# Graph attention layers on one Trainium2 core: the softmax weights move from the one-hots into the gathered rows and the edge features

## The reference

```python
def _gat_layer(x, src, dst, edge_attr_full, W, att, b, ew, eb):
    edge_emb = edge_attr_full @ ew.T + eb
    xw = x @ W
    xj = xw[src].reshape(-1, H, D) + edge_emb.reshape(-1, H, D)
    xi = xw[dst].reshape(-1, H, D)
    ...
    alpha = ea / (denom[dst] + EPS)
    msg = xj * alpha[..., None]
    aggr = jax.ops.segment_sum(msg, dst, num_segments=N)
    return aggr.mean(axis=1) + b
```

## Time and profile before

| | |
|---|---|
| time, median of 3 runs | 5991.09 us (5987.72 to 5996.44) |
| span of the profiled execution | 6300.0 us |
| PE busy | 5130.7 us, 81% |
| PE weight loads busy | 4275.1 us, 68% |
| DVE busy | 4152.4 us, 66% |
| ACT busy | 3248.8 us, 52% |
| POOL busy | 2967.6 us, 47% |
| the five attention layers | about 1790 to 4130 us of the span |

### The profile page before, as it was taken

One profiled execution on the slowest core, in us unless ns is written; L12 is line 12 of the kernel. 1 busy time (PEld: TensorE's weight loads), 2 busy tenths in 40 slices (PEclk: granted clock), 3 DMA queues, 4 the chain that ended last, 5 costly groups with the idle time before them and its releaser, 6 DMA issues. The chain is left out here.

```text
span 6300.0 us, 105600 instructions
## 1 busy us (share of the span) xinstructions
PE 5130.7 (81%) x29899; PEld 4275.1 (68%) x29899; DVE 4152.4 (66%) x16499; ACT 3248.8 (52%) x8537; POOL 2967.6 (47%) x2871
## 2 busy tenths in 40 slices
PE   4888998889959969969969969977795757758655
PEld 3666666667749959959959958844575646646555
DVE  4666776678856657757757757778475647737754
ACT  1667777777735535535535535534573325646400
POOL 1655665555564334334334335312561346545366
PEclk6999999999979979979979979955897768989855
DMA  2988776555535435535535535458573446745332
GB/s 72 176 182 185 193 191 189 185 186 196 192 100 119 109 68 118 110 67 116 113 66 115 113 69 122 110 171 250 130 155 80 137 117 187 206 108 113 65 86 79
DMA packets 1227633, 841.35 MB, mean 134 GB/s; under 512 B 335962, under 2 KB 1188542, under 8 KB 1226736
## 3 DMA queue, kind: packets, MB, share of 16 engines
q1 hardware_dynamic: 1146756, 706.02, 43.4%
q0 software_dynamic: 77040, 128.08, 9.5%
q10 hardware_dynamic: 3264, 0.50, 0.0%
HBM read 390.57 MB, written 448.11 MB: 133 GB/s over the span
## 5 line engine op out<-in xcount | busy, mean ns | idle before, releaser
L747 POOL DMA_INDIRECT gat_G<-table,k_src_row x980 | 958.2, 978 | 903.8 <-PE gat_psE L1515 688.5
L1437 ACT ACTIVATE gat_aggT<-gat_psG 128x512 f32<-128x512 f32 x490 | 292.5, 597 | 656.5 <-PE gat_psE L1515 573.2
L1510 PE MATMUL gat_psG<-gat_S,gat_G 128*128 128x256 f32 x1960 | 602.8, 390 | 31.4 <-issue 19.8
L1515 PE MATMUL gat_psE<-gat_S,gat_exr 128*128 128x128 f32 x3920 | 607.3, 278 | 0.0
L451 POOL TENSOR_TENSOR nodes_rstd<-nodes_var,k_half 128x14 f32<-128x14 f32 x138 | 360.4, 2612 | 517.8 <-DVE nodes_var L511 514.4
L1302 DVE TENSOR_SCALAR gat_S<-k_iota,k_endpos,gat_al 128x128 f32<-128x128 f32 x1960 | 551.0, 342 | 59.0 <-issue 38.4
L1515 PEld LDWEIGHTS gat_psE<-gat_S,gat_exr 128*128 128x128 f32 x3920 | 524.5, 195 | 0.0
L1526 PE MATMUL gat_psZ<-gat_aggT,t_gat_wh 128*128 128x256 f32 x1960 | 508.3, 382 | 2.7 <-ACT gat_hT L1444 1.3
L1512 PE MATMUL gat_psG<-k_ident,gat_loop 128*128 128x128 f32 x1960 | 379.6, 276 | 0.0
L1526 PEld LDWEIGHTS gat_psZ<-gat_aggT,t_gat_wh 128*128 128x128 f32 x1960 | 336.4, 192 | 32.0 <-ACT gat_aggT L1437 2.9
L1444 ACT ACTIVATE gat_hT<-gat_psZ,t_gat_bias 128x256 f32<-128x256 f32 x490 | 231.9, 473 | 239.1 <-issue 137.0
(11 more groups left out here) (650 smaller groups left out, 14567.1 us busy)
## 6 DMA issues: line engine op xcount, KB each, us to landing
table<-nodes_rows SPq DMA_DIRECT2D x660, 198.0 KB
table<-nodes_n SPq DMA_DIRECT2D x396, 192.0 KB
gat_own<-table SPq DMA_DIRECT2D x490, 132.0 KB
table<-gat_rows SPq DMA_DIRECT2D x392, 132.0 KB
nodes_x<-in_x SPq DMA_DIRECT2D x132, 192.0 KB
out<-nodes_x_out SPq DMA_DIRECT2D x132, 192.0 KB
gat_exr<-in_ex_pad SPq DMA_DIRECT2D x70, 336.0 KB
gat_G<-table,k_src_row POOLq DMA_INDIRECT x980
```

The costliest lines, as they stand in the source:

```text
L747: eng.indirect_dma_start(to, None, table, bass.IndirectOffsetOnAxis(ap=index, axis=0)).then_inc(sem, 16)
L1437: eng.activation(aggT[:, i % RA, :, :, :].rearrange("p t h q -> p (t h q)"), psG[i % 2][:, :], ACT.Copy).then_inc(s.aggT, 1)
L1510: eng.matmul(o, G[:, g % RG, c, 0:D], S[:, i % RS, t, :, :].rearrange("p h q -> p (h q)"), start=True, stop=False)
L1515: mm = eng.matmul(psE[i % 2][:, t * P:(t + 1) * P], exr[:, g % 2, c, (1 - h) * EDGE_F:(1 - h) * EDGE_F + P], S[:, i % RS, t, h, :], start= ...
```

## The change

The one-hot of a tile, `ends_at`, no longer carries the weight and is made once for both heads; a pair's two come from one DVE instruction of 128x256. The weights are multiplied into the gathered rows instead (`Gw`, one DVE instruction of 128x512 a pair: two tiles, two heads) and, once a group, into the edge features (`wex`, one DVE instruction of 128x448, in `weighed_features`, issued ahead of the group's first pair). A tile's two heads stand side by side in the 32 columns of `wex`, so one product of 128 columns replaces the two on the edge features. On the rows, two products of 128 columns (one a head, each with its own stationary `Gw`) replace the one of 256. The edge features are loaded into a tile of their own, `ex`, which is contiguous in a partition; its buffer comes free when `wex` has been computed, and `wex` itself when the group before last has been aggregated. The first `aggregate` of a group waits for `wex` rather than for the load.

```diff
-        exr = A.sb("exr", [P, 2, GM, P + EDGE_F])
-        S, loop = A.sb("S", [P, RS, 2, H, P]), A.sb("loop", [P, RS, 2, H, P])
+        ex, wex = A.sb("ex", [P, 2, GM, 3 * EDGE_F]), A.sb("wex", [P, 2, GM, P])
+        ends_at, Gw, loop = A.sb("ends_at", [P, RS, 2, P]), A.sb("Gw", [P, RS, 2, H, P]), A.sb("loop", [P, RS, 2, H, P])
...
-                        eng.wait_ge(s.agg, PG * (g - 1))
+                        eng.wait_ge(s.wex, g - 1)
...
-                    eng.dma_start(exr[:, j, :, 0:3 * EDGE_F], I.ex_pad[:, g * GM:(g + 1) * GM, :]).then_inc(ex_in[j], 16)
+                    eng.dma_start(ex[:, j, :, :], I.ex_pad[:, g * GM:(g + 1) * GM, :]).then_inc(ex_in[j], 16)
...
-                eng.memset(exr[:, :, :, 3 * EDGE_F:P + EDGE_F], 0.0).then_inc(s.padded, 1)
+                eng.memset(wex[:, :, :, E2:P], 0.0).then_inc(s.padded, 1)
...
+                def weighed_features(g):
+                    eng.wait_ge(s.al, g + 1)
+                    eng.wait_ge(ex_in[g % 2], 16 * uses(g, 2))
+                    if g >= 2:
+                        eng.wait_ge(s.agg, PG * (g - 1))
+                    a = al[:, g % 2, 0, :].rearrange("p (h t) -> p t h", h=H)
+                    eng.tensor_tensor(wex[:, g % 2, :, 0:E2].rearrange("p t (h f) -> p t h f", h=H),
+                                      spread(ex[:, g % 2, :, EDGE_F:2 * EDGE_F], 2, H), spread(a, 3, EDGE_F), ALU.mult
+                                      ).then_inc(s.wex, 1)
+
                 def one_hot(i):
                     g, k = divmod(i, PG)
                     if k == 0:
-                        eng.wait_ge(s.al, g + 1)
+                        weighed_features(g)
                     if i >= RS:
                         eng.wait_ge(s.agg, i - RS + 1)
-                    for t in range(2):
-                        for h in range(H):
-                            a = h * GM + 2 * k + t
-                            ins = eng.tensor_scalar(S[:, i % RS, t, h, :], K.iota[:, :], K.endpos[:, 2 * i + t:2 * i + t + 1],
-                                                    al[:, g % 2, 0, a:a + 1], ALU.is_equal, ALU.mult)
-                    ins.then_inc(s.S, 1)
+                    eng.tensor_tensor(ends_at[:, i % RS, :, :], spread(K.iota[:, :], 1, 2), spread(K.endpos[:, 2 * i:2 * i + 2], 2, P),
+                                      ALU.is_equal)
+                    a = al[:, g % 2, 0, :].rearrange("p (h t) -> p t h", h=H)[:, 2 * k:2 * k + 2, :]
+                    eng.tensor_tensor(Gw[:, i % RS, :, :, :], spread(G[:, g % RG, 2 * k:2 * k + 2, 0:D], 2, H), spread(a, 3, D), ALU.mult
+                                      ).then_inc(s.weighed, 1)
...
                     if k == 0:
-                        eng.wait_ge(ex_in[g % 2], 16 * uses(g, 2))
+                        eng.wait_ge(s.wex, g + 1)
...
-                        eng.matmul(o, G[:, g % RG, c, 0:D], S[:, i % RS, t, :, :].rearrange("p h q -> p (h q)"), start=True, stop=False)
                         for h in range(H):
+                            eng.matmul(o[:, h * P:(h + 1) * P], Gw[:, i % RS, t, h, :], ends_at[:, i % RS, t, :], start=True, stop=False)
                             eng.matmul(o[:, h * P:(h + 1) * P], loop[:, i % RS, t, h, :], K.ident[:, :], is_transpose=True,
-                                       start=False, stop=(h == H - 1))
-                        for h in range(H):
-                            mm = eng.matmul(psE[i % 2][:, t * P:(t + 1) * P], exr[:, g % 2, c, (1 - h) * EDGE_F:(1 - h) * EDGE_F + P], S[:, i % RS, t, h, :],
-                                            start=(h == 0), stop=(h == H - 1))
+                                       start=False, stop=True)
+                        mm = eng.matmul(psE[i % 2][:, t * P:(t + 1) * P], wex[:, g % 2, c, :], ends_at[:, i % RS, t, :],
+                                        start=True, stop=True)
```

More of the change, by code:

```diff
@@ L1125, in gat_layer @@
             "seq", "fill_out", "fill_in", "ox_in", "sq", "scores_turned", "step", "to_exp", "exped", "alphas", "alphas_turned", "al",
-            "S", "loop1", "loop0", "agg", "aggT", "aggE", "mixed", "hT", "rowed", "rows_done", "pieces", "sc", "st_in",
+            "weighed", "wex", "loop1", "loop0", "agg", "aggT", "aggE", "mixed", "hT", "rowed", "rows_done", "pieces", "sc", "st_in",
             "weights", "weights_turned", "wc", "px", "pe", "pie_turned", "pieE_turned", "pr", "prE", "comb", "summed", "aggX", "zx",
@@ L1498, in aggregate @@
                     g, k = divmod(i, PG)
-                    eng.wait_ge(s.S, i + 1)
+                    eng.wait_ge(s.weighed, i + 1)
                     eng.wait_ge(s.loop1, i + 1)
```

## The result

The changed kernel takes 5826.65 us in the median of 4 runs (5823.05 to 5835.43), the kernel before 5990.99. The ratio is 0.9719, 95% interval 0.9708 to 0.9730: faster by 164 us. Predicted were 5823 us.

What follows compares the result with a forecast made beforehand. PE's streamed moving columns bound the layers: 81 of 98 pairs a layer save 0.42 us, 34.0 us less 0.5, so 168 us over five layers. From 5991 that gives 5823 us, range 5764 to 5880.

Steps and rivals of the forecast that it cites:

- PE is the bound, and moving columns are its price: Inside the layers PE streams fewer columns: 0.21 us less a tile, 0.42 us less a pair.
- neither bound (0.85, 0.90): PE's eight records a tile at 0.107 or 0.113 us each: gain of 0.24 or 0.20 us a tile.
- The rule on weight loads: Rival: PE's weight loads set the pace, gain between nothing and 0.37 us a pair; taken at 5991 us, chance 4%.
- The turnings take a part back: PE waits for `alB` at 13 weight turnings a layer, losing 0.42 us each; a group takes 25.84 us.
- The end of a layer takes two pairs back: PE waits for DVE's chain over the crossing nodes, so the last two pairs' saving, 0.84 us, is lost.
- The start of a layer: Two pairs' saving counted lost where engines idle on issue; features lie open before the first aggregation, 0.5 us a layer.
- The gathers: POOL's gathers keep a mean below 1 us; two a pair at 0.97 us, 1.9 us, cost 0.
- the rival that DVE's products hinder POOL: DVE and POOL hinder each other: work 1.6 times as long, half the gain lost, 8%; doubled, 6043 us, 4%.
- DVE: New DVE work a pair about 0.95 us, features 0.65 a group; waits of 0.3 and 3.7 us stay, not the bound.
- The rival's price: DVE's new work 1.6 times as long uses up its 4.0 us slack a group: 84 us lost, 5907 us, 8%.
- The row I had set against it: Profile row cited against DVE and POOL hindering: a product beside a gather takes 0.42 us, the gather 0.97.

Runs made afterwards that it cites:

- e4: Changed kernel with a second product on the edge features (zero stationary tile, two more records of 128 columns a tile) put back for PE alone: 6011.55 us, ratio 1.0026.
- e2: Changed kernel with the edge features loaded into a tile of the old width, so in small packets again: 5819.47 us, ratio 0.9709.
- e1: The kernel before, unchanged, profiled once more: 5997.08 us, ratio 1.0005.
- e5: Changed kernel with a group's exponential moved ahead in ACT's queue, in front of pair 4's eviction: 5799.28 us, ratio 0.9673.
- e7: Changed kernel with the product of the gathered rows made twice on DVE, once into a tile nobody reads: 5890.44 us, ratio 0.9823.
- e3: Only the edge feature part of the change; weighted one-hots stay for the gathered rows, an unweighted one is made beside them: 5830.34 us, ratio 0.9724.

## Why the prediction was right, point by point

- **PE is the bound, and moving columns are its price.** Right. The tile was put at 0.89 us and is 0.89, the pair at 3.52 and is 3.52; e4 takes the gain away with PE's two records alone, and e2 shows that the packets of the feature load have no part in it. The trace agrees with neither bound (0.85, 0.90) but with the value between.
- **The rule on weight loads.** The changed kernel has the same loads (29,899 in both pages). In the window from 2200 to 2480 us they are busy for 253.27 of 280 us in e1 and for 262.43 after. The forecast of that rule was at most 0.37 us a pair; 0.42 were gained. Here the start-to-start time of the records decided, not the share of the loads.
- **The turnings take a part back.** Right in kind, a little large in size. I let 0.42 us go at each turning and had 25.84 us for a group; it is 25.74, because the wait is 0.33 us (e5). The missing 0.1 was slack: `alB` ended at 2510.25 and PE came at 2510.38, so PE could come about that much earlier before it had to wait. I had called both paths equally long.
- **The end of a layer takes two pairs back.** Right to 0.01 us in the trace (0.50 to 1.34); in the time it is too small to be seen.
- **The start of a layer.** Wrong in mechanism and too small, made good by the slack at the turnings: that the sum came out is luck here. I wrote off two pairs (0.84 us) and 0.5 us for the features in a stretch of idle issue, which e1 doesn't have. The features do lie open: the first aggregation follows the weights' copy by 2138.70 - 2136.25 = 2.45 us after, and by 2170.90 - 2168.87 = 2.03 in e1. But from the first copy of the weights to the second, where a group later saves 2.62 us, layer 0 goes from 27.32 to 27.60 us, and the five layers together from 130.3 to 127.8: 2.1 us a layer are lost, not 1.3. There PE's saving runs into the wait for the second group's gathers, which moreover land later after the change (next point). Per layer the sum was 33.5 us; measured in layer 0 were 460.8 - 427.1 = 33.7, made of 12 x 2.62 = 31.4 for the later groups and 2.5 behind the last turning, less 0.3 in the first.
- **The gathers.** I expected their mean to stay below 1 us, leaning on one gather beside one product. It rose from 982 to 1052 ns after and to 1310 in e7. In the later groups POOL has room for that, at a layer's start it hasn't: there it issues gathers without a pause, and each delay moves all that follow. Timelines of POOL and DVE in layer 0, the 23rd and 24th gather and the first instruction that needs the second group's rows, in e1 and then after:

```profile
1705.59 0.94 POOL L747 DMA_INDIRECT gat_G<-table,k_src_row  x1 [0.30 <-issue]
1706.84 1.01 POOL L747 DMA_INDIRECT gat_G<-table,k_src_row  x1 [0.30 <-issue]
1714.50 0.20 DVE L1236 TENSOR_TENSOR gat_sq<-gat_G,t_edge_sc 128x28 f32<-128x28 f32 x1 [3.14 <-DMA gat_G<-table,k_src_row]
```

```profile
1706.60 1.39 POOL L747 DMA_INDIRECT gat_G<-table,k_src_row  x1 [0.30 <-issue]
1708.29 1.96 POOL L747 DMA_INDIRECT gat_G<-table,k_src_row  x1 [0.30 <-issue]
1717.11 0.20 DVE L1236 TENSOR_TENSOR gat_sq<-gat_G,t_edge_sc 128x28 f32<-128x28 f32 x1 [4.62 <-DMA gat_G<-table,k_src_row]
```

  Counted from the start of the layer's second memset (1679.95 and 1681.04), DVE gets the second group's rows after 34.55 us in e1 and after 36.07 in the changed kernel, 1.5 us later. It is DVE's new work and not PE's speed that does it: e4, in which PE is as slow as before, has 36.02 us and the longer first group. Nor is it the form of the feature load: DVE's waits for gathers sum to 88.9 us in e2 as in after, and to 82.0 in e1. e3, without the product of the rows, lies between (35.17). So the rival that DVE's products hinder POOL was partly true; over the five layers the rows come 0.9 to 1.7 us later, some 7 us in all, which is my estimate of its price.
- **DVE.** Durations right: features 0.62 (0.65 predicted), comparison and product 0.94 (0.95). Its room was wrong. I counted its idle time, 4.0 us a group, and asked whether the new work fits into that. But the sum of the scores must be ready for PE after pair 1, and by the timeline of after it ends at 2322.99 and is turned at 2324.48: 1.5 us of room over the first four pairs, not 4.0 over seven. In e7 four pairs with 0.60 us more each need 2.4, and PE waits 0.82. The forecast was untouched, since the change needs none of it. The rival's price (84 us at 0.57 us more a pair and 0.4 for the features) is near the 64 us of e7, but its own sum doesn't give it: 4.4 us of work less 4.0 of room is 0.4 us a group, 26 us in all. The same count gave e7's forecast of 0 to 10 us.

## What to carry to other kernels

Where TensorE is the bound, count streamed columns and ask what each operand forces to be streamed twice: one unweighted one-hot for all heads let two products share their columns, and half of this change (the features alone) brought its gain, whole within the noise. A step on the bound engine that is as long as a chain beside it (here the turning of the weights, the end of the layer) gives nothing when it gets shorter; find these first, they say what is to be moved next, and a queue order may give the loss back for free. An engine's idle time isn't its room: for each result that the bound engine takes from it, measure from when it is ready to when it is needed. The same holds for the gathers, which had room in the middle of a layer and none at its start.

## What the runs showed of the hardware

Products of two tensors on DVE lengthen the gathers issued by POOL, and are not lengthened themselves. With DVE running such products back to back (e7), single gathers took 1.84 and 2.10 us where they take 0.94 to 0.95 otherwise; the 128x512 product stayed at a mean of 675 ns in after and in e7, and between 671 and 692 ns in all of its instructions. That is the contention of which the Trainium skill speaks (GPSIMD Engine Reference, Key points: instructions with two SBUF inputs); the trace agrees with the rule, and adds that the gather pays for it. The row I had set against it was a single gather beside a single product, too little to see it.

The granted clock in the window from 2200 to 2480 us stayed at 1.00 (2.4 GHz) although PE now idles 0.33 us once a group. At the start of layer 1, where PE has stood for 9.68 us before the first turning, its first aggregation runs at a granted clock of 0.50 (1.2 GHz) with 0.21 us a record, in e1 and after alike.
